# Dissolving the coefficient stage of a graph network kernel into the first softmax

## The chip, the cores and the metric

The kernel runs on one core of one Trainium2 chip. The metric is device time in microseconds of one execution. The kernel before took 5043.83 us, the median of three runs (5041.87 to 5056.84). Engines are named as the profile names them: PE multiplies matrices, DVE is the vector engine, ACT the scalar engine, POOL the GpSimd engine, SP issues DMAs.

## The reference

Four graph layers run over one graph of 50,000 nodes with 128 features and 25,000 edges sorted by destination; each adds its result to its input and normalises it. The first is a three-layer attention network with four heads, then two graph convolutions and a SAGE layer. What the change touches are these lines:

```python
logits = leaky_relu(a_s[src] + a_d[dst] + ew[:, None], 0.2)     # attention; ew: mean of the embedded edge features
                                                                 # self edges take the mean of ew over all edges
deg  = segment_sum(w, col)                                       # convolution 1: weighted degree, self loop of weight 1
dis  = where(deg > 0, rsqrt(deg), 0)
norm = dis[row] * w * dis[col]
deg  = segment_sum(ones, col); norm = rsqrt(deg)[row] * rsqrt(deg)[col]   # convolution 2
m    = segment_sum(h[src], dst) / maximum(deg, 1)                # SAGE
```

## The kernel before, in words

Edges are padded to 25,088 and lie in 196 tiles of 128 slots, 49 batches of four tiles; 98 rows of 256 slots are the second layout of the same edges, in which the softmax scans along the free axis. Nodes are 98 batches of 512.

`program` (line 128) calls one stage after the other: `edge_structure`, `layer_weights`, `node_chain`, `first_slots`, `coefficients`, then `edge_scores(0)`, `softmax(0)`, `attend(0)`, the same three for layers 1 and 2, and five `convolve` stages. Each stage is a block in which every engine has its own instruction list in the order written; lists wait for each other only by semaphores. At a stage's end the semaphores are cleared and all engines meet at a barrier (line 117), so nothing of a stage starts before everything of the stage ahead has ended.

`coefficients` (lines 502 to 555) works alone between two barriers. Its inputs are `ew` (the edges' mean embeddings, [128, 3, 196], for three layers) and `node_map`, which holds for each slot the row number, the weighted degree, the plain degree and a spare column for the edge's source (`src_map`) and for its destination (`dst_map`); one node_map entry is 16 bytes. DVE sums `ew` and adds the bias mean `be1`; PE turns `ew` into the row layout (six transposes) and sums it over partitions with a matrix of ones; DVE rounds the source rows to integers (`src_row`, the gather indices), then makes the masks, one reciprocal, waits for ACT's square root of all degrees, takes their reciprocal, multiplies them into `meta` (coefficients `coef[0..2]` and the self-loop ones), and last writes `ew_mean` and the three `ew_rows` from PSUM.

`edge_scores(0)` gathers source rows with 196 indirect DMAs that POOL issues (line 1434) by `src_row`, paced by PE's progress. `softmax(0)` (line 1756) is a chain on DVE: SP loads the self scores and the edge scores; POOL adds `ew_rows` to the edge scores (line 1834); DVE runs segmented maxima and sums by scans forward (line 274) and backward (line 279), with two short turns through PE (lines 299, 301) in each of three rounds, masks and joins (line 291), and ends with reciprocals and products into `meta` (lines 1899, 1902). `attend(0)` copies `meta` for each batch. The coefficients are first read by the `convolve` stages.

Of the kernel before, what the change touches and what calls it, by code (L numbers as in the profile page):

```python
# [8 lines left out]
F32 = mybir.dt.float32  # L9
I32 = mybir.dt.int32  # L10
ALU = mybir.AluOpType
ACT = mybir.ActivationFunctionType
AX = mybir.AxisListType

P = 128
# [8 lines left out]
ROW = 256  # L24
QUAD = P // GB
STEP = QUAD // HEADS
KEY, COEF, SELF, ALPHA = 2, 3, 6, 8
# [120 lines left out]
def program(nc, io, n_nodes, n_edges):  # L148
    nb, n_slots, n_rows_nodes = sizes(n_nodes, n_edges)
    n_tiles = nb * GB  # L150
    n_rows = n_slots + n_rows_nodes
    rq = n_tiles // 2
    ctx = ExitStack()
    with ctx:
# [16 lines left out]
        ident = sb("ident", [P, P])  # L171
# [3 lines left out]
        src_row = sb("src_row", [P, n_tiles], I32)  # L175
# [3 lines left out]
        meta = sb("meta", [P, n_tiles, 12])  # L179
        w_edge = sb("w_edge", [DE, 3])  # L180
        be1 = sb("be1", [P, 3])
        ones = sb("ones", [P, P])
        ew_rows = sb("ew_rows", [rq, 3, ROW])
# [126 lines left out]
        def edge_structure():  # L310

            with ExitStack() as c, Semaphores(nc) as sem:
# [23 lines left out]
                with nc.Block() as block:  # L336
# [68 lines left out]
                    def _(dve):  # L405
# [92 lines left out]
                        st(nc.vector.tensor_scalar(w_edge[:, :], w_edge[:, :], 1.0 / D, None, ALU.mult))  # L498
                        st(nc.vector.tensor_reduce(be1[:, :], bem[:, :, :], AX.X, ALU.add))
                        st(nc.vector.tensor_scalar(be1[:, :], be1[:, :], 1.0 / D, None, ALU.mult))  # L500

        def coefficients():

            with ExitStack() as c, Semaphores(nc) as sem:
                ew_sum = c.enter_context(nc.sbuf_tensor("ew_sum", [P, 4], F32))
                chain, roots, to_pe, turned = (sem(x) for x in ("chain", "roots", "to_pe", "turned"))
                deg, pos_deg = node_map[:, :, :, 1:3], node_map[:, :, :, 3]
                coef = [meta[:, :, COEF + k] for k in range(3)]
                with nc.Block() as block:
                    @block.scalar  # L510
                    def _(act):
                        act.wait_ge(roots, 1)
                        nc.scalar.sqrt(deg, deg).then_inc(roots, 1)

                    @block.tensor
                    def _(pe):
                        pe.wait_ge(to_pe, 1)
                        nc.tensor.matmul(bank[7][:, 0:3], ones[:, :], ew_sum[:, 0:3], start=True, stop=True)
                        for k in range(3):
                            for j in range(2):  # L520
                                ins = nc.tensor.transpose(bank[k][0:rq, j * P:(j + 1) * P],
                                                          ew[:, k, :].rearrange("p (q j) -> p j q", j=2)[:, j, :], ident[:, :])
                        ins.then_inc(turned, 1)

                    @block.vector
                    def _(dve):
                        st = Chain(dve, chain).step

                        st(nc.vector.tensor_reduce(ew_sum[:, 0:3], ew[:, :, :], AX.X, ALU.add))
                        for k in range(3):  # L530
                            st(nc.vector.tensor_scalar(ew[:, k, :], ew[:, k, :], be1[:, k:k + 1], None, ALU.add))
                        dve.sem_inc(to_pe, 1)
                        st(nc.vector.tensor_copy(src_row[:, :], src_map[:, :, 0]))

                        w_deg = node_map[:, :, :, 1]
                        st(nc.vector.tensor_scalar(pos_deg, w_deg, 0.0, None, ALU.is_gt))
                        st(nc.vector.tensor_tensor(w_deg, w_deg, pos_deg, ALU.mult))
                        st(nc.vector.scalar_tensor_tensor(w_deg, w_deg, 1.0, pos_deg, ALU.add, ALU.subtract))

                        st(nc.vector.tensor_scalar(coef[2], dst_map[:, :, 2], 1.0, 1.0, ALU.subtract, ALU.max))  # L540
                        st(nc.vector.reciprocal(coef[2], coef[2]))
                        dve.sem_inc(roots, 1)
                        dve.wait_ge(roots, 2)
                        st(nc.vector.reciprocal(deg, deg))
                        st(nc.vector.tensor_tensor(w_deg, w_deg, pos_deg, ALU.mult))
                        for k in range(2):
                            st(nc.vector.tensor_tensor(coef[k], src_map[:, :, 1 + k], dst_map[:, :, 1 + k], ALU.mult))
                            st(nc.vector.tensor_tensor(meta[:, :, SELF + k], dst_map[:, :, 1 + k], dst_map[:, :, 1 + k], ALU.mult))
                        st(nc.vector.tensor_tensor(coef[0], coef[0], w_part[:, :], ALU.mult))
                        dve.wait_ge(turned, 1)  # L550
                        st(nc.vector.scalar_tensor_tensor(ew_mean[:, :], bank[7][:, 0:3], 1.0 / n_edges, be1[:, :],
                                                          ALU.mult, ALU.add))
                        for k in range(3):
                            st(nc.vector.tensor_copy(ew_rows[:, k, :], bank[k][0:rq, 0:ROW]))

        def layer_weights(w_first, b_first, beta_col, bias):

# [669 lines left out]
        def edge_scores(l, first, second, t_in, t_mid, t_out, start, end, solo=False):  # L1227
# [3 lines left out]
            with ExitStack() as c, Semaphores(nc) as sem:  # L1231
# [15 lines left out]
                if first:  # L1247
# [13 lines left out]
                sc_stored = [sem(f"sc_stored{r}") for r in range(4)]  # L1261
                x_in, mid_stored, z_stored = ([[sem(f"{n}{h}{r}") for r in range(4)] for h in range(2)] for n in (
                    "x_in", "mid_stored", "z_stored"))
                w_in, tails_out, banks_open, sp_pace, dve_pace = (sem(x) for x in ("w_in", "tails_out", "banks_open", "sp_pace", "dve_pace"))
                n_w = 4 if first else 2
                b_t = bank[0:2]
# [13 lines left out]
                with nc.Block() as block:  # L1280
# [115 lines left out]
                    def _(pool):  # L1396
                        def pace(b, g):
# [20 lines left out]
                            else:  # L1418
                                pool.wait_ge(turned, 2 * b - 1)

                        if patch:
                            for k in range(n_tails):
                                n = min(P, n_tiles - k * P)
                                nc.gpsimd.indirect_dma_start(
                                    out=tails[k][0:n, :], out_offset=None, in_=tables[l].slots,
                                    in_offset=bass.IndirectOffsetOnAxis(ap=tail_index[0:n, k:k + 1], axis=0)).then_inc(tails_in, 16)
                            pool.wait_ge(tails_out, 16 * n_tails)
# [379 lines left out]
        def softmax(layer):  # L1807

            with ExitStack() as c, Semaphores(nc) as sem:  # L1810
# [5 lines left out]
                                     "self_ready", "less_max", "edge_exp", "self_exp"))  # L1816
                summed, edge_turned, sum_turned = (sem(x) for x in ("summed", "edge_turned", "sum_turned"))

                def head_columns(h, j):
                    at = ((h % 2) * 2 + j) * rq  # L1820
                    return slice(at, at + rq)
                with nc.Block() as block:
                    @block.sync
                    def _(sp):
                        for j in range(2):
                            sp.dma_start(sr[:, :, j * P:(j + 1) * P], score_rows(self_score, j)).then_inc(self_in, 16)
                        for j in range(2):
                            sp.dma_start(lr[:, :, j * P:(j + 1) * P], score_rows(edge_score, j)).then_inc(edge_in, 16)

                    @block.gpsimd  # L1830
                    def _(pool):
                        pool.wait_ge(edge_in, 32)
                        for h in range(HEADS):
                            ins = nc.gpsimd.tensor_tensor(lr[:, h, :], lr[:, h, :], ew_rows[:, layer, :], ALU.add)
                        ins.then_inc(edge_ready, 1)

                    @block.scalar
                    def _(act):
                        act.wait_ge(shift_made, 1)
                        act.wait_ge(self_spread, 1)  # L1840
                        for h in range(HEADS):
                            ins = nc.scalar.activation(sr[:, h, :], seg_f[:, h, :], ACT.Identity, bias=shift[0:rq, h:h + 1])
                        ins.then_inc(self_ready, 1)
                        act.wait_ge(less_max, 1)
                        nc.scalar.activation(lr[:, :, :], lr[:, :, :], ACT.Exp).then_inc(edge_exp, 1)
                        act.wait_ge(less_max, 2)
                        nc.scalar.activation(sr[:, :, :], sr[:, :, :], ACT.Exp).then_inc(self_exp, 1)

                    @block.tensor
                    def _(pe):  # L1850
                        for n, what in enumerate(("max", "max", "sum")):
                            run_totals_pe(pe, ends_made, turned, n, what)
                        pe.wait_ge(edge_exp, 1)
# [14 lines left out]
                    def _(dve):  # L1868
                        ch = Chain(dve, chain)
                        st = ch.step  # L1870
                        nc.vector.scalar_tensor_tensor(shift[:, :], att_shift[:, layer, :], -1.0,
                                                       ew_mean[:, layer:layer + 1].to_broadcast([P, HEADS]),
                                                       ALU.mult, ALU.add).then_inc(shift_made, 1)
# [1094 lines left out]
                node_chain(w_first, b_first, beta_col, bias)  # L2968
            first_slots(w_first, b_first, beta_col)
        raw_early.close()  # L2970
        coefficients()
        edge_scores(0, (io["L1_gnn_W1"], io["c_L1_gnn_b1"]), (io["L1_gnn_W2"], io["b_L1_gnn_b2"]), t[3], t[4], t[5], 0, nb)
        softmax(0)
        attend(0)
# [76 lines left out]
```

## Time and profile before

| | |
|---|---|
| median of three runs | 5043.83 us |
| profiled execution, its own time | 5052.05 us |
| its span | 5049.9 us |
| PE busy | 3969.3 us (79%) |
| DVE busy | 3727.1 us (74%) |
| ACT busy | 3450.8 us (68%) |
| POOL busy | 3018.4 us (60%) |
| `coefficients`, from DVE's first instruction to the next stage's first | 1199.76 to 1218.40 us |
| `softmax(0)`, from barrier to barrier | 1606.19 to 1661.94 us |

The share of busy time says little here: the span is a row of stages with barriers between them, and each stage has its own limit. For this change the timeline of two short stretches is what counts. A row of the timeline gives start, duration, engine, line, operation, what is written from what, partitions by elements, how many instructions were merged, and in brackets the engine's idle time before it and what ended that.

### The profile page before, as it was taken

What the parts mean: (1) busy time and instruction counts of PE and PEld (TensorE: products, weight loads), DVE (VectorE), ACT (ScalarE), POOL (GpSimd) and SP (SyncE); (2) the same over time, 40 slices, a digit from 0 to 9 for tenths busy, and PEclk for the clock granted to TensorE, in tenths of its full rate; (3) what the DMA queues carried; (4) which work ended last, traced back from release to release, by engine and by line L of the source; (5) the groups of instructions that cost most, each with busy time, mean ns of one, the idle gap of its engine ahead of it and who ended that gap; (6) DMA issues with size and microseconds to landing.
All of it is one profiled execution on the core that took longest, in us unless ns stands there. A gap on an engine that the chain in (4) does not pass through costs nothing. (4 is left out here: it accounts for less than half of the span.)

```text
span 5049.9 us, 108087 instructions
## 1 busy us (share of the span) xinstructions
PE 3969.3 (79%) x24378; PEld 2916.8 (58%) x24378; DVE 3727.1 (74%) x14651; ACT 3450.8 (68%) x11317; POOL 3018.4 (60%) x2914
## 2 busy tenths in 40 slices
PE   1999999797996898994998974997877666666554
PEld 1667667565774454873555752444766565665554
DVE  4899999545998787897886966997668787544433
ACT  0789999554886676894776863887878787333332
POOL 6888888255452122761224462887757676767777
PEclk9999999798998899997998997998998898997666
DMA  2566666487996576994777984775766565543332
GB/s 90 157 186 200 196 195 197 161 308 258 351 349 220 196 240 203 357 362 146 241 242 243 333 305 141 228 227 169 234 202 208 187 210 187 153 145 115 93 101 70
DMA packets 603571, 1061.32 MB, mean 210 GB/s; under 512 B 109737, under 2 KB 124603, under 8 KB 603373
## 3 DMA queue, kind: packets, MB, share of 16 engines
q1 hardware_dynamic: 521644, 920.61, 53.4%
q0 software_dynamic: 81728, 138.51, 10.6%
q8 instruction: 70, 1.15, 0.1%
q14 instruction: 129, 1.05, 0.1%
HBM read 608.75 MB, written 453.92 MB: 210 GB/s over the span
## 5 line engine op out<-in xcount | busy, mean ns | idle before, releaser
L2540 POOL DMA_INDIRECT got_c<-table,src_row x980 | 931.4, 950 | 387.7 <-issue 311.9
L1434 POOL DMA_INDIRECT src_got_s<-table,src_row x588 | 554.6, 943 | 445.9 <-issue 93.0
L2572 PE MATMUL bank<-pick_c,got_c 128*128 128x128 f32 x1960 | 333.3, 323 | 352.9 <-DMA got_c<-table,src_row 281.5
L2082 PE MATMUL bank<-w_all,dt_m 128*128 128x512 f32 x1176 | 569.2, 601 | 35.2 <-DMA dt_m<-delta_t 34.0
L2572 PEld LDWEIGHTS bank<-pick_c,got_c 128*128 128x128 f32 x1960 | 288.1, 226 | 396.5 <-issue 244.6
L2056 POOL TENSOR_TENSOR part_m<-part_m,half_sum_m 128x512 f32<-128x512 f32 x98 | 158.6, 1619 | 581.8 <-DVE half_sum_m L2289 581.8
L1607 ACT ACTIVATE z_s<-z_s,shift_s,dev_s 128x128 f32<-128x128 f32 x1080 | 444.0, 485 | 2.2 <-DVE shift_s L1745 1.3
L793 PEld LDWEIGHTS bank<-w_mean,ht 128*128 128x128 f32 x2352 | 312.1, 193 | 142.5 <-issue 142.5
L2596 PE MATMUL bank<-w_c,agg_c 128*128 128x128 f32 x1960 | 370.5, 315 | 4.0 <-ACT agg_c L2717 3.8
L2717 ACT COPY agg_c<-bank 128x512 f32<-128x512 f32 x245 | 142.8, 583 | 320.3 <-DVE bank L1920 274.5
L790 PE MATMUL bank<-bias,first_row 128*128 128x512 f32 x588 | 321.3, 628 | 38.0 <-ACT ht L853 13.8
L2082 PEld LDWEIGHTS bank<-w_all,dt_m 128*128 128x128 f32 x1176 | 210.2, 193 | 231.1 <-issue 133.7
L2596 PEld LDWEIGHTS bank<-w_c,agg_c 128*128 128x128 f32 x1960 | 325.1, 230 | 19.8 <-issue 11.5
L843 ACT ACTIVATE bank<-bank 128x128 f32<-128x128 f32 x1176 | 306.8, 261 | 42.0 <-PE bank L793 33.9
L2183 ACT ACTIVATE part_m<-bank,now_m 128x128 f32<-128x128 f32 x588 | 215.0, 366 | 157.7 <-PE bank L2082 141.2
L793 PE MATMUL bank<-w_mean,ht 128*128 128x128 f32 x2352 | 313.2, 277 | 0.0
L2728 ACT ACTIVATE z_c<-z_c,shift_c,dev_c 128x128 f32<-128x128 f32 x588 | 242.2, 482 | 89.0 <-DVE shift_c L2868 89.0
L2832 DVE TENSOR_SCALAR pick_c<-iota,now_c 128x128 f32<-128x128 f32 x980 | 282.3, 365 | 11.8 <-DVE now_c L2828 0.5
L754 POOL TENSOR_TENSOR rows<-rows 128x512 f32<-128x512 f32 x196 | 260.5, 1329 | 42.9 <-DVE rows L925 40.7
L2061 POOL DMA_INDIRECT x_m<-in_x_dram,dst_node x196 | 222.0, 1133 | 98.5 <-issue 52.0
L1913 DVE COPY tails_c<-tails_c 128x1 f32<-128x1 f32 x245 | 37.5, 153 | 328.4 <-PE bank L2572 322.5
L2289 DVE SCALAR_TENSOR_TENSOR part_m<-bank,now_m,part_m 128x128 f32<-128x128 f32 x588 | 203.6, 346 | 69.5 <-ACT half_sum_m L2184 68.2
(352 smaller groups left out, 11912.6 us busy)
## 6 DMA issues: line engine op xcount, KB each, us to landing
table<-rows SPq DMA_DIRECT2D x294, 256.0 KB
x_s<-table SPq DMA_DIRECT2D x270, 256.0 KB
x_c<-table SPq DMA_DIRECT2D x245, 256.0 KB
table<-z_s SPq DMA_DIRECT2D x196, 256.0 KB
table<-z_c SPq DMA_DIRECT2D x196, 256.0 KB
table<-mid_s SPq DMA_DIRECT2D x172, 256.0 KB
own_rows_s<-table SPq DMA_DIRECT2D x147, 256.0 KB
pick_t_s<-picks_t SPq DMA_DIRECT2D x147, 256.0 KB
```

What stands on the lines that cost most here:

```text
L754: nc.gpsimd.tensor_tensor(flat(rows[l + 1][r]), flat(rows[l + 1][r]), flat(rows[l][r]), ALU.add).then_inc(summed[l], 1)
L790: nc.tensor.matmul(b_y[l][:, :], first_row[:, :], bias[:, l, :, :].rearrange("p g d -> p (g d)"), start=True, stop=False, skip_group_check ...
L793: ins = nc.tensor.matmul(b_y[l][:, g * D:(g + 1) * D], ht[l][b.half][:, g, :], w_mean[:, l, :], start=False, stop=True, skip_group_check=True)
L843: ins = nc.scalar.activation(bank[7][:, g * D:(g + 1) * D], b_y[l][:, g * D:(g + 1) * D], ACT.Square, accum_out=square[l][r][:, g:g + 1])
L1434: nc.gpsimd.indirect_dma_start(out=src_got[r][:, g, :], out_offset=None, in_=tables[l].rows, in_offset=bass.IndirectOffsetOnAxis(ap=src_ro ...
L1607: ins = nc.scalar.activation(v[:, g, :], v[:, g, :], ACT.Identity, bias=shift[side(b, h)][:, g:g + 1], scale=dev[side(b, h)][:, g:g + 1])
L2082: nc.tensor.matmul(b_h[k % n_h][:, :], dt[b.slot][:, k, :], w_all[:, l, :, :].rearrange("p h d -> p (h d)"), start=True, stop=True).then_i ...
L2540: nc.gpsimd.indirect_dma_start(out=got[r][:, g, :], out_offset=None, in_=t_in.rows, in_offset=bass.IndirectOffsetOnAxis(ap=src_row[:, t:t ...
L2572: ins = nc.tensor.matmul(b_sum[r][:, k * P:(k + 1) * P], got[b.slot][:, k, :], pick[r][:, k, :], start=k == 0, stop=sage, skip_group_check ...
L2596: ins = nc.tensor.matmul(b_y[r][:, k * D:(k + 1) * D], agg[r][:, k, :], ws[0][:, :], start=False, stop=True, skip_group_check=True)
L2728: ins = nc.scalar.activation(z[b.slot][:, g, :], z[b.slot][:, g, :], ACT.Identity, bias=shift[r][:, g:g + 1], scale=dev[r][:, g:g + 1])
L2832: ins = nc.vector.tensor_scalar(pick[r][:, k, :], iota[:, :], now[r][:, k, KEY:KEY + 1], now[r][:, k, COEF + m:COEF + m + 1], ALU.is_equal ...
```

## The change

`coefficients` is no longer a stage. Its parts go to two later ones:

- In `edge_scores(0)` POOL makes `src_row` itself, waits for it, and then issues the gathers.
- At the head of `softmax(0)` DVE sums `ew` and adds `be1`, PE multiplies and turns into banks 7 and 4 to 6, ACT (instead of DVE) copies the three `ew_rows` out of PSUM, DVE makes `ew_mean`. POOL waits for ACT's copies before its four adds.
- Behind these adds POOL computes all of the degree arithmetic. There is no square root and no reciprocal any more: five tensor_tensor instructions raise to a power, with an exponent of -1 or -0.5 read from a two-column tensor `powers` and broadcast. Each step waits for the one before by a semaphore.

```diff
@@ edge_scores, POOL
+                        if l == 0:
+                            nc.gpsimd.tensor_copy(src_row[:, :], src_map[:, :, 0]).then_inc(rows_known, 1)
+                            pool.wait_ge(rows_known, 1)
@@ softmax, POOL
+                        if layer == 0:
+                            pool.wait_ge(ew_out, 1)
                         pool.wait_ge(edge_in, 32)
                         for h in range(HEADS):
                             ins = nc.gpsimd.tensor_tensor(lr[:, h, :], lr[:, h, :], ew_rows[:, layer, :], ALU.add)
                         ins.then_inc(edge_ready, 1)
+                        if layer == 0:
+                            st = Chain(pool, coef_chain).step
+                            st(nc.gpsimd.memset(powers[:, 0:1], -1.0))
+                            st(nc.gpsimd.memset(powers[:, 1:2], -0.5))
+                            st(nc.gpsimd.tensor_scalar(coef[2], dst_map[:, :, 2], 1.0, 1.0, ALU.subtract, ALU.max))
+                            st(nc.gpsimd.tensor_tensor(coef[2], coef[2], powers[:, 0:1].to_broadcast([P, n_tiles]), ALU.pow))
+                            st(nc.gpsimd.tensor_scalar(pos_deg, w_deg, 0.0, None, ALU.is_gt))
+                            st(nc.gpsimd.tensor_tensor(w_deg, w_deg, pos_deg, ALU.mult))
+                            st(nc.gpsimd.tensor_scalar(w_deg, w_deg, 1.0, None, ALU.add))
+                            st(nc.gpsimd.tensor_tensor(w_deg, w_deg, pos_deg, ALU.subtract))
+                            for part in (src_map, dst_map):
+                                for k in range(2):
+                                    st(nc.gpsimd.tensor_tensor(part[:, :, 1 + k], part[:, :, 1 + k], powers[:, 1:2].to_broadcast([P, n_tiles]), ALU.pow))
+                            st(nc.gpsimd.tensor_tensor(w_deg, w_deg, pos_deg, ALU.mult))
+                            for k in range(2):
+                                st(nc.gpsimd.tensor_tensor(coef[k], src_map[:, :, 1 + k], dst_map[:, :, 1 + k], ALU.mult))
+                                st(nc.gpsimd.tensor_tensor(meta[:, :, SELF + k], dst_map[:, :, 1 + k], dst_map[:, :, 1 + k], ALU.mult))
+                            st(nc.gpsimd.tensor_tensor(coef[0], coef[0], w_part[:, :], ALU.mult))
@@ softmax, ACT
+                        if layer == 0:
+                            act.wait_ge(ew_turned, 1)
+                            for k in range(3):
+                                ins = nc.scalar.copy(ew_rows[:, k, :], bank[4 + k][0:rq, 0:ROW])
+                            ins.then_inc(ew_out, 1)
@@ softmax, PE
+                        if layer == 0:
+                            pe.wait_ge(ew_ready, 2)
+                            nc.tensor.matmul(bank[7][:, 0:3], ones[:, :], ew_sum[:, 0:3], start=True, stop=True)
...
+                            ins.then_inc(ew_turned, 1)
@@ softmax, DVE
+                        if layer == 0:
+                            nc.vector.tensor_reduce(ew_sum[:, 0:3], ew[:, :, :], AX.X, ALU.add).then_inc(ew_ready, 1)
+                            dve.wait_ge(ew_ready, 1)
+                            for k in range(3):
+                                ins = nc.vector.tensor_scalar(ew[:, k, :], ew[:, k, :], be1[:, k:k + 1], None, ALU.add)
+                            ins.then_inc(ew_ready, 1)
+                            dve.wait_ge(ew_turned, 1)
+                            st(nc.vector.scalar_tensor_tensor(ew_mean[:, :], bank[7][:, 0:3], 1.0 / n_edges, be1[:, :],
+                                                              ALU.mult, ALU.add))
@@ program
-        coefficients()
```

POOL in the first softmax, before (L1834 is the add of `ew_rows`, the rows under it end the stage):

```order
L1830 UNCONDITIONAL_BRANCH
L1834 TENSOR_TENSOR edge_r<-edge_r,ew_rows 98x256 x4
L1822 UNCONDITIONAL_BRANCH
L116 ISA
```

```order
L1794 TENSOR_TENSOR edge_r<-edge_r,ew_rows 98x256 x4
L1798 MEMSET powers 128x1
L1799 MEMSET powers 128x1
L1800 ISA
L1800 TENSOR_SCALAR meta<-node_map 128x196
L1801 TENSOR_TENSOR meta<-meta,powers 128x196
L1802 TENSOR_SCALAR node_map<-node_map 128x392
L1803 TENSOR_TENSOR node_map<-node_map 128x392
L1804 TENSOR_SCALAR node_map<-node_map 128x392
L1805 TENSOR_TENSOR node_map<-node_map 128x392
L1808 TENSOR_TENSOR node_map<-node_map,powers 128x196 x4
L1809 TENSOR_TENSOR node_map<-node_map 128x392
```

Sixteen instructions that read the tensors stand behind the adds where there were none; the last five, not shown, are the products L1811 to L1813.

DVE at the head of the first softmax now (before, `self_shift` was its first instruction there, and the three rows ahead of it stood in the coefficient stage):

```order
L1858 UNCONDITIONAL_BRANCH
L1863 TENSOR_REDUCE ew_sum<-ew 128x3
L1866 TENSOR_SCALAR ew<-ew,be 128x196 x3
L1869 SCALAR_TENSOR_TENSOR ew_mean<-bank,be 128x3
L1871 SCALAR_TENSOR_TENSOR self_shift<-att_shift,ew_mean 128x4
L1875 TENSOR_TENSOR self_r<-self_r,tail_bound 98x1024
```

Five DVE instructions come ahead of `self_shift`, the last of them behind a round through PE.

## Rows read from the trace of the kernel before

**Rows 1.** Timeline, the coefficient stage and both barriers around it.
```profile
1196.64 0.50 SPq L1097 DMA_DIRECT2D self_score<-slot_scores  x1
1199.76 0.77 DVE L529 TENSOR_REDUCE ew_sum<-ew 128x3 f32<-128x588 f32 x1 [4.23 <-PEq L117]
1200.56 1.04 DVE L531 TENSOR_SCALAR ew<-ew,be 128x196 f32<-128x196 f32 x3
1201.71 0.50 PEld L518 LDWEIGHTS bank<-ew_sum,ones 128*128 128x128 f32 x2 [6.83 <-DVEq L532]
...
1202.16 1.50 PE L521 MATMUL bank<-ident,ew 128*98 128x128 f32 x6
...
1207.26 5.05 DVE L544 RECIPROCAL node_map<-node_map 128x784 f32<-128x784 f32 x1 [1.01 <-ACT node_map L513]
...
1216.15 1.34 DVE L554 COPY ew_rows<-bank 98x256 f32<-98x256 f32 x3
1218.40 0.20 ACT L1579 ACTIVATE warm<-eps 128x1 f32<-128x1 f32 x1 [11.17 <-SPq L117]
...
1219.04 0.94 POOL L1434 DMA_INDIRECT src_got_s<-table,src_row  x1 [35.79 <-POOLq L117]
```

**Rows 2.** Timeline, first use of a gathered row in edge_scores(0).
```profile
1229.80 1.05 PE L1493 MATMUL bank<-own_rows_s,pick_t_s 128*128 128x128 f32 x8
...
1230.97 0.69 DVE L1712 TENSOR_TENSOR delta_s<-src_got_s,bank 128x512 f32<-128x512 f32 x1 [2.99 <-PE bank L1493]
```

**Rows 3.** Timeline, the head of softmax(0).
```profile
1606.19 1.83 SPq L1826 DMA_DIRECT2D self_r<-self_score  x2
1606.23 0.16 DVE L1871 SCALAR_TENSOR_TENSOR self_shift<-att_shift,ew_mean 128x4 f32<-128x4 f32 x1 [5.44 <-PEq L117]
1608.06 0.94 SPq L1828 DMA_DIRECT2D edge_r<-edge_score  x2
1610.70 1.23 DVE L1875 TENSOR_TENSOR self_r<-self_r,tail_bound 98x1024 f32<-98x1024 f32 x1 [4.31 <-DMA self_r<-self_score]
1611.96 3.88 DVE L274 TENSOR_TENSOR_SCAN seg_f<-pen,self_r 98x256 f32<-98x256 f32 x4
1612.28 4.08 POOL L1834 TENSOR_TENSOR edge_r<-edge_r,ew_rows 98x256 f32<-98x256 f32 x4 [41.08 <-DMA edge_r<-edge_score]
1615.87 2.78 DVE L279 TENSOR_TENSOR_SCAN seg_b<-pen,seg_f 98x256 f32<-98x256 f32 x4
```

**Rows 4.** Windows over edge_scores' and softmax(0)'s stretches: busy time, instructions, granted clock.
```profile
1199.80:1217.50 17.70, 1.94 (x8) 1.48 (x8) 15.90 (x21) 0.89 (x1) 0.00 (x0) 0.50 0.00 0
1217.50:1230.00 12.50, 6.53 (x16) 3.60 (x17) 0.69 (x1) 1.38 (x3) 8.48 (x9) 0.55 0.75 249
1617.00:1661.00 44.00, 4.99 (x22) 3.32 (x22) 39.43 (x68) 5.10 (x7) 0.00 (x0) 0.50 0.00 0
```

**Rows 5.** Lines L274 and L1834: durations in ns, min/median/max.
```profile
L274 DVE TENSOR_TENSOR_SCAN seg_f<-pen,self_r x12: 665/1140/1162, 1612.0 to 3078.6; 98x256 f32<-98x256 f32 x12
L274 DVE TENSOR_TENSOR_SCAN seg_f<-pen,edge_r x12: 666/666/691, 1626.3 to 3092.0; 98x256 f32<-98x256 f32 x12
L1834 POOL TENSOR_TENSOR edge_r<-edge_r,ew_rows x12: 717/1100/1165, 1612.3 to 3079.2; 98x256 f32<-98x256 f32 x12
```

**Rows 6.** Timeline, a DVE instruction beside a POOL add in node_chain.
```profile
186.73 1.70 POOL L754 TENSOR_TENSOR rows<-rows 128x512 f32<-128x512 f32 x1 [0.41 <-DVE rows L925]
...
187.31 1.14 DVE L980 SCALAR_TENSOR_TENSOR shiftn<-statn,devn 128x4 f32<-128x4 f32 x1
```

**Rows 7.** Lines L980, L925 and L754: durations in ns, min/median/max.
```profile
L980 DVE SCALAR_TENSOR_TENSOR shiftn<-statn,devn x98: 123/125/1143, 168.8 to 956.8; 128x4 f32<-128x4 f32 x98
L925 DVE SCALAR_TENSOR_TENSOR rows<-bank,devn,gamma_w x784: 329/336/353, 114.1 to 933.8; 128x128 f32<-128x128 f32 x196
L754 POOL TENSOR_TENSOR rows<-rows x196: 1263/1288/1707, 124.4 to 934.2; 128x512 f32<-128x512 f32 x196
```

**Rows 8.** Timeline, the end of softmax(0) and the start of attend(0).
```profile
1659.63 1.31 DVE L1902 TENSOR_TENSOR meta<-bank,inverse 128x196 f32<-128x196 f32 x2
1661.94 1.28 ACT L2173 ACT_TABLE_LOAD   x1 [20.56 <-PEq L117]
```

More of the change, by code:

```diff
@@ L500, in _ @@
                         st(nc.vector.tensor_scalar(be1[:, :], be1[:, :], 1.0 / D, None, ALU.mult))
[L502 to L554, printed above, removed]
@@ L1263, in edge_scores @@
                     "x_in", "mid_stored", "z_stored"))
+                rows_known = sem("rows_known")
                 w_in, tails_out, banks_open, sp_pace, dve_pace = (sem(x) for x in ("w_in", "tails_out", "banks_open", "sp_pace", "dve_pace"))
@@ L1817, in softmax @@
                 summed, edge_turned, sum_turned = (sem(x) for x in ("summed", "edge_turned", "sum_turned"))
+                if layer == 0:
+                    powers = c.enter_context(nc.sbuf_tensor("powers", [P, 2], F32))
+                    ew_sum = c.enter_context(nc.sbuf_tensor("ew_sum", [P, 4], F32))
+                    ew_ready, ew_turned, ew_out, coef_chain = (sem(x) for x in (
+                        "ew_ready", "ew_turned", "ew_out", "coef_chain"))
+                    deg, pos_deg, w_deg = node_map[:, :, :, 1:3], node_map[:, :, :, 3], node_map[:, :, :, 1]
+                    coef = [meta[:, :, COEF + k] for k in range(3)]
                 def head_columns(h, j):
@@ L1850, in _ @@
                     def _(pe):
+                        if layer == 0:
+                            pe.wait_ge(ew_ready, 2)
+                            nc.tensor.matmul(bank[7][:, 0:3], ones[:, :], ew_sum[:, 0:3], start=True, stop=True)
+                            for k in range(3):
+                                for j in range(2):
+                                    ins = nc.tensor.transpose(bank[4 + k][0:rq, j * P:(j + 1) * P],
+                                                              ew[:, k, :].rearrange("p (q j) -> p j q", j=2)[:, j, :], ident[:, :])
+                            ins.then_inc(ew_turned, 1)
                         for n, what in enumerate(("max", "max", "sum")):
@@ L1870, in _ @@
                         st = ch.step
+                        if layer == 0:
+                            nc.vector.tensor_reduce(ew_sum[:, 0:3], ew[:, :, :], AX.X, ALU.add).then_inc(ew_ready, 1)
+                            dve.wait_ge(ew_ready, 1)
+                            for k in range(3):
+                                ins = nc.vector.tensor_scalar(ew[:, k, :], ew[:, k, :], be1[:, k:k + 1], None, ALU.add)
[3 more added lines that the diff above has]
+                                                              ALU.mult, ALU.add))
                         nc.vector.scalar_tensor_tensor(shift[:, :], att_shift[:, layer, :], -1.0,
```

## The prediction

> **What bounds the kernel now.** The page's chain of waits follows only the last convolution stage and its busy shares are spread over unlike stages, so I read the timeline around the two places that the change touches. There the reader sees a row of stages with barriers. In the coefficient stage DVE works alone: 15.90 us busy of 17.70, PE 1.94, ACT 0.89, POOL and DMA nothing [rows 4]; every microsecond of it is on the path. In softmax(0), behind 1617 us, DVE is busy 39.43 of 44.00 us and POOL not at all [rows 4]: that stage is DVE's chain, and its idle POOL is where the work goes.
>
> **What goes away.** The stage begins for DVE at 1199.76 and the next one for ACT at 1218.40 [rows 1]. All of it goes, one barrier with it: 18.64 us. PE's clock changes nothing: it is granted 0.50 in the coefficient stage and 0.55 just behind [rows 4], so PE starts edge_scores at the lower level (1.2 GHz) in both kernels.
>
> **src_row on POOL.** DVE's cast of 196 elements goes with the stage. POOL's copy has no row; it reads less than the add of 98x256, 0.72 us at its fastest [rows 5], and the wait behind it adds little, so the 196 gathers start about 0.7 us later (0.3 to 1.5). The first gathered row is used at 1230.97, by an instruction that waited for PE [rows 2], while the first gather went out at 1219.04 [rows 1]: the four of batch 0 take about 5 us, landing some us more, and several us of cover remain. Cost 0; without that cover 0.7 us.
>
> **The head of softmax(0).** DVE waited 4.31 us for the self scores, until 1610.70 [rows 3]. New ahead of `self_shift` are the sum and the three adds, which ran from 1199.76 to 1201.60, then PE, whose last transpose ended at 1203.66 [rows 1]: 3.90 us. From the barrier at 1606.23 that is 1610.13; `ew_mean` and `self_shift` at 0.16 us each and their waits end it near 1610.55, 0.1 us before the scores are there. Cost 0, with bounds of 0 and 0.5. ACT's three copies cannot cost DVE's 1.34 us [rows 1] by much more, so `ew_rows` stands by about 1611.6, ahead of POOL's start at 1612.28 [rows 3]. Cost 0, bounds 0 and 0.7.
>
> **POOL's arithmetic.** It runs from 1616.4 (the last add's end) and must be done when DVE is, at 1660.94 [rows 8]. So 44.5 us of time stand open on POOL. The question is what it does to DVE meanwhile.
>
> The trace shows a price [rows 5]. The scans that run beside POOL's adds take 1140 ns in the median, the same scans without them 666; POOL's add goes from 717 to 1100. How it comes about is seen in node_chain [rows 6, 7]: a DVE instruction of 4 elements, 125 ns normally, took 1140 ns and ended at 188.45, when POOL's add, begun at 186.73, had just ended (188.43). It stood still behind a whole POOL instruction. L925, which reads one operand from PSUM, never takes over 353 ns [rows 7]. So a DVE instruction that reads two operands from SBUF waits for a POOL instruction that reads SBUF, to its end. In softmax(0) nearly all of DVE's chain is of this kind (scans, joins, maxima, differences). The Trainium skill states the same as a rule (SBUF — State Buffer, Who interferes with whom): the port pair is an exclusive lock held for the whole instruction, so whoever comes second stands still. It speaks against this change: POOL is idle there, yet its time isn't free.
>
> So each POOL instruction costs DVE about its own streaming time. An add of 256 elements holds about 0.53 us: the difference of the two fastest adds, 1263 and 717 ns for 512 and 256 elements [rows 7, 5], is 2.1 ns an element. Behind the adds stand:
> - two-input plain ones: three of 392 and five of 196 elements, 2,156 x 2.1 ns = 4.5 us;
> - one-input ones: 196 + 2 x 392 = 980 elements at about half, 1.1 us;
> - five powers of 196 elements.
> The plain ones hold 5.6 us. The skill has a rule for these strided operands too (GPSIMD Engine Reference, Performance pitfalls: steps over 8 bytes cost about half more); by it they would be 8.4 us; no row shows it.
>
> No row shows a power on POOL. Lowest: the price of a product, 0.41 us each, 2 us for five. The other end I work out as a program: logarithm, product, exponential are some 30 arithmetic steps; were each as dear as a whole element of an add, 30 x 2.1 = 63 ns an element, 12.3 us an instruction and 62 us for five. An add's element is mostly reading and writing, its arithmetic perhaps a third, which gives 21 ns, 4.1 us each, 20.5 us for five; for comparison, DVE's reciprocal takes 6.4 ns an element [rows 1]. I take 4.1.
>
> DVE's loss is then 5.6 + 20.5 = 26.1 us, less the share that falls on its rounds through PE and its PSUM reads, about 15%: 22.2 us. POOL itself ends near 1616.4 + 5.6 + 20.5 + 16 steps' gaps and waits for DVE (about 10) = 1652.5, before DVE at 1660.9 + 22.2: its own end isn't late. A reload of POOL's library stands ahead of the first tensor_scalar; it falls in POOL's slack. The skill (GPSIMD Engine Reference, Instruction dispatch) puts some 6 us on a freshly loaded kernel's first call; no run here shows it, and by it POOL would still end first.
>
> **Sum.** -18.64 + 0 + 0 + 22.2 = +3.6 us. Against the profiled execution's 5052.05 that is 5055.7. That execution lies 8.2 us over the median of the runs, so I put the difference on the median: 5043.83 + 3.6 = 5047. A measurement of this kernel can hardly tell less than 0.3%, 15.1 us, from no change.
>
> **Rivals.**
> - Slower: the power is dear. Each ns per element of it costs 0.98 us in all, about 0.85 of it on DVE. From 31 ns an element (6 us an instruction) on, the sum passes +15. At the upper end, 63 ns, DVE stands still nearly the whole 62 us: -18.64 + 0.9 x (62 + 5.6) = +42 us, 5086; at twice that, powers taken by code that isn't pipelined, +97, where POOL's end passes DVE's. For it: five times 196 powers in software, and a row that shows whole-instruction blocking. Against it: nothing measured.
> - Faster: POOL's work is hidden after all, because a power computes long and reads little and lets DVE in between, or costs next to nothing, and its plain steps fall on DVE's rounds through PE. The loss must stay under 3.5 us: 5025 to 5029. For it: 44.5 us of open time. Against it: the blocking [rows 5 to 7]; with blocking, even powers at the price of a product leave (5.6 + 2) x 0.8 = 6 us of loss and -12.6 us, 5031, still within 0.3%.
> - The change doesn't do what it says: the head of softmax(0) runs late by the PE round and the ACT copies (1.2 us), or a different wait keeps most of the 18.64 us. 0.5 to 1.2 us only; it moves no case to another.
>
> **How the numbers follow.** The forecast is "within 0.3%" with 5047: powers from 0.4 to 6 us give -12.6 to about +14, its own range 5031 to 5058. Chance 0.47. The slower rival 0.40, the faster one 0.13 (with the third inside these). For 8 in 10 I leave out the lower half of the faster case and the slower case's far tail: 5028 to 5100.
>
> **What the profile after would show.** No DVE row between the last stores of first_slots and the load of edge_scores; ACT's `warm` some 18.6 us earlier. In softmax(0) the tensor_tensor on self_r still at about 4.5 us behind the barrier, its wait ended by the self scores. POOL busy behind its adds with five rows that name `powers`: their duration is the term I know least. Beside them DVE's scans over 666 ns, up to a power's own duration. A scan that keeps 666 ns beside a power refutes the blocking. Softmax(0) longer by about 22 us. The prediction is wrong if softmax(0) grows by less than 3.5 us or more than 34.

## The result and the profile after

The changed kernel takes 5157.07 us (median of four runs, 5148.34 to 5165.25) where the kernel before takes 5046.0 (5041.87 to 5056.84): a ratio of 1.0216, 95% interval 1.0193 to 1.0240. That is 111 us slower; 5047 was forecast, with a range of 5028 to 5100. (The ratios here and below are estimated from all runs of both kernels, and can differ by some 0.1% from the quotient of the two medians.) The kernel is slower beyond doubt; whether by more than 2% the interval leaves open.

The timeline shows the two places where the change acts. First the end of first_slots and the start of edge_scores(0) in the changed kernel (start, duration, engine, line, operation; in brackets the idle time before it), which answers to [rows 1]:

```profile
1180.16 0.50 SPq L1043 DMA_DIRECT2D self_score<-slot_scores  x1
1183.23 0.34 SPq L1230 DMA_DIRECT2D w_s<-in_L_gnn_W_dram  x1
1183.25 0.20 ACT L1529 ACTIVATE warm<-eps 128x1 f32<-128x1 f32 x1 [4.23 <-PEq L117]
1183.27 0.52 POOL L1369 CAST src_row<-node_map 128x196 int32<-128x196 f32 x1 [19.22 <-POOLq L117]
...
1184.06 0.96 POOL L1384 DMA_INDIRECT src_got_s<-table,src_row  x1 [0.27 <-POOL src_row L1369]
```

From the last store's start to ACT's `warm` are 3.09 us; before they were 1218.40 - 1196.64 = 21.76 [rows 1]. So 18.67 us went, as forecast. The gathers start 0.81 us behind `warm` instead of 0.64, and edge_scores(0), from `warm` to the next stage's first load, takes 386.3 us (387.8 before).

Then softmax(0), whose head answers to [rows 3] and whose last row answers to [rows 8]:

```profile
1569.57 0.87 SPq L1784 DMA_DIRECT2D self_r<-self_score  x2
1569.61 0.77 DVE L1863 TENSOR_REDUCE ew_sum<-ew 128x3 f32<-128x588 f32 x1 [5.43 <-PEq L117]
...
1573.23 0.92 ACT L1820 COPY ew_rows<-bank 98x256 f32<-98x256 f32 x3 [7.38 <-PE bank L1839]
...
1573.43 0.16 DVE L1871 SCALAR_TENSOR_TENSOR self_shift<-att_shift,ew_mean 128x4 f32<-128x4 f32 x1
1574.75 1.23 DVE L1875 TENSOR_TENSOR self_r<-self_r,tail_bound 98x1024 f32<-98x1024 f32 x1 [1.16 <-DMA self_r<-self_score]
...
1582.08 32.04 POOL L1801 TENSOR_TENSOR meta<-meta,powers 128x196 f32<-128x196 f32 x1
1582.33 1.01 DVE L279 TENSOR_TENSOR_SCAN seg_b<-pen,seg_f 98x256 f32<-98x256 f32 x1
...
1590.99 2.44 DVE L274 TENSOR_TENSOR_SCAN seg_f<-pen,edge_r 98x256 f32<-98x256 f32 x4
...
1621.06 127.72 POOL L1808 TENSOR_TENSOR node_map<-node_map,powers 128x196 f32<-128x196 f32 x4
...
1624.94 1.32 DVE L1902 TENSOR_TENSOR meta<-bank,inverse 128x196 f32<-128x196 f32 x2
...
1753.05 0.69 POOL L1813 TENSOR_TENSOR meta<-meta,w_part 128x196 f32<-128x196 f32 x1
1754.74 1.28 ACT L2173 ACT_TABLE_LOAD   x1 [148.68 <-PEq L117]
```

A power of 196 elements takes 32 us on POOL. DVE is done at 1626.26, then everyone waits for POOL until 1753.74. From the first load to the next stage's first instruction the stage lasts 185.17 us; before it lasted 55.75 [rows 3, 8]. The balance, +129.4 - 18.7 = +110.7 us, accounts for the 111 between the medians. The two profiled executions themselves are only 96.7 us apart (spans of 5146.6 and 5049.9): the stages ahead, which the change leaves alone, happened to end 16.5 us earlier in the changed kernel's (last store at 1180.16 instead of 1196.64), and what follows softmax(0) took 3.9 us more. So the agreement to 1 us is partly luck; the two lengths above are read inside their stages and don't hang on it.

Two windows, DVE's chain and what is behind it, show who works (the columns are, as in [rows 4]: length, then busy time and instructions of PE, weight loads, DVE, ACT and POOL, the granted clock, the DMA share and GB/s):

```profile
1570.00:1626.30 56.30, 6.93 (x30) 4.80 (x30) 48.42 (x80) 6.02 (x10) 49.37 (x13) 0.50 0.05 15
1626.30:1754.00 127.70, 0.00 (x0) 0.00 (x0) 0.00 (x0) 0.00 (x0) 126.74 (x10) 0.50 0.00 0
```

And DVE isn't slower beside a power: the four scans at 1590.99 take 2.44 us in the middle of one, what the four took before with POOL idle. Only the scan that was issued at the power's start is longer, 1.01 us instead of 0.66 [rows 5]. That refutes the second half of my argument. DVE's chain, from the first load to its last product, takes 56.69 us; before, 54.75. The 1.9 us are 0.7 at the head (the self scores are there 5.2 us behind the load instead of 4.5), 0.6 in the backward scans and 0.6 in the last joins, beside a tensor_scalar of POOL.

### The profile page after: what moved, and what is told of

Read it like the earlier page. It is cut to its first block and busy times, and to the rows that moved or that the text cites. A ratio compares the mean times of both kernels' runs of the same rounds, so it can differ in the third digit from the quotient of the medians.

```text
span 5146.6 us, 108068 instructions
## 1 busy us (share of the span) xinstructions
PE 3930.7 (76%) x24378; PEld 2882.0 (56%) x24378; DVE 3697.7 (72%) x14635; ACT 3449.3 (67%) x11319; POOL 3155.3 (61%) x2933
## 5 line engine op out<-in xcount | busy, mean ns | idle before, releaser
L2596 PE MATMUL bank<-w_c,agg_c 128*128 128x128 f32 x1960 | 353.5, 304 | 5.2 <-ACT agg_c L2717 5.1
L2596 PEld LDWEIGHTS bank<-w_c,agg_c 128*128 128x128 f32 x1960 | 309.7, 220 | 22.1 <-issue 11.5
L2061 POOL DMA_INDIRECT x_m<-in_x_dram,dst_node x196 | 190.2, 970 | 98.4 <-POOLq L117 46.6
```

The costliest lines, as they stand in the source:

```text
L2596: ins = nc.tensor.matmul(b_y[r][:, k * D:(k + 1) * D], agg[r][:, k, :], ws[0][:, :], start=False, stop=True, skip_group_check=True)
```

## The experiments

Theory A, formed from these rows: the loss is the powers' own length, nothing else; beside them DVE runs free. Against it stood B (the new order, the head or the waits cost) and the theory on record, that every POOL instruction which reads SBUF stops DVE for its whole length. The length of softmax(0) below is always from SP's first load to ACT's first row of the next stage. The edits are shown abridged, some lines of them in words.

### Products in place of the powers

```diff
-...to_broadcast([P, n_tiles]), ALU.pow))
+...to_broadcast([P, n_tiles]), ALU.mult))
```

> The changed kernel with each of the five powers turned into a product of the same shape, so the degree powers and coefficients are not computed. Theory A (the powers' own length is the whole loss; beside them DVE runs free): softmax(0) falls from 185.2 us to 57 to 61 us, its end set by DVE again, POOL's sixteen instructions done in about 17 us, and the kernel takes 14 to 17 us less than before (about 5030). Theory B (the loss is the new order: waits, the barrier behind POOL, the head of the stage): softmax(0) stays over 80 us and the kernel is slower than before.

The kernel leaves out the powers, so it doesn't compute the coefficients; it serves for the time alone. 5041.75 us against 5051.87 of before, measured together, ratio 0.9984 (0.9970 to 0.9999): 10 us less by the medians, where 14 to 17 were expected. The rows of its softmax(0):

```profile
1581.64 0.85 SPq L1784 DMA_DIRECT2D self_r<-self_score  x2
...
1601.06 2.87 POOL L1808 TENSOR_TENSOR node_map<-node_map,powers 128x196 f32<-128x196 f32 x4
...
1606.85 4.29 DVE L274 TENSOR_TENSOR_SCAN seg_f<-pen,edge_r 98x256 f32<-98x256 f32 x4
...
1644.66 1.28 ACT L2173 ACT_TABLE_LOAD   x1 [20.58 <-PEq L117]
```

The stage lasts 63.02 us, 122 less than with powers and 7.3 more than before; 57 to 61 was expected, so A's "nothing else" is too strong. B falls as the cause of the loss: the same list in the same order, with products for powers, isn't slower than before. But the plain instructions do cost: the four scans that took 2.44 us now take 4.29. Of the eleven plain instructions the changed kernel ran one ahead of the first power, four beside the last 12 us of DVE's chain, where it mostly waits and reads PSUM, and the six products behind its end; here nearly all run beside scans and joins.

### Powers as logarithm and exponential on ACT

```diff
+ # POOL: masks ahead of its adds, then products once ACT is done
+ # ACT, behind the copies of ew_rows:
+ act.wait_ge(masked, 1)
+ nc.scalar.activation(coef[2], coef[2], ACT.Ln)
+ nc.scalar.activation(deg, deg, ACT.Ln).then_inc(logged, 1)
+ act.wait_ge(logged, 1)
+ nc.scalar.activation(coef[2], coef[2], ACT.Exp, scale=-1.0)
+ nc.scalar.activation(deg, deg, ACT.Exp, scale=-0.5).then_inc(raised, 1)
```

> The changed kernel with the masks on POOL ahead of its adds, and the powers made by ACT as a logarithm and an exponential (784 and 196 elements each), where ACT waits for DVE's first round; only the six products stay on POOL behind the adds. Theory A: ACT needs about 5 us with two table loads (the later table load for the softmax's Exp goes away), all beside DVE; softmax(0) takes 57 to 61 us and the kernel 14 to 17 us less than before. Theory B (any of this work in softmax(0) costs, since POOL's plain instructions stop DVE): softmax(0) over 64 us, gain under 10 us.

5038.28 us, ratio 0.9978 (0.9966 to 0.9989): the first complete version whose whole interval lies below the time before, by 0.1 to 0.3%. ACT's four instructions and both table loads take 6.1 us and end at 1600.52, 11.6 us behind the stage's first load:

```profile
1588.93 0.85 SPq L1783 DMA_DIRECT2D self_r<-self_score  x2
...
1596.96 0.89 ACT L1819 ACTIVATE node_map<-node_map 128x784 f32<-128x784 f32 x1
1597.87 1.28 ACT L1821 ACT_TABLE_LOAD   x1
...
1599.62 0.90 ACT L1822 ACTIVATE node_map<-node_map 128x784 f32<-128x784 f32 x1
1600.20 4.38 DVE L279 TENSOR_TENSOR_SCAN seg_b<-pen,seg_f 98x256 f32<-98x256 f32 x4
...
1648.44 1.28 ACT L2174 ACT_TABLE_LOAD   x1 [20.60 <-PEq L117]
```

The stage lasts 59.51 us, within what A expects. The 3.8 us over before lie beside POOL's plain instructions: 2.3 in the first eight scans, such as the 4.38 us above, which were 2.78 before [rows 3], 0.9 at the head beside the masks, and 0.5 in a copy of four columns.

### Powers and long adds of chosen shapes

```diff
+ # before's kernel, behind the adds; results unused
+ softmax(0): 5 x tensor_tensor(probe, flat_w, flat_w, ALU.add)      # 128x1536
+ softmax(1): tensor_tensor(..., ALU.pow) on 128x384, 128x196, 128x98, 128x49
+ softmax(2): pow on 128x98 (exponent 2), 128x98 (base 1.0), 64x98, 16x98, 8x98, 1x98, 128x196 (exponent 2)
```

> The kernel before with added POOL instructions on scratch tensors behind the adds, results unused: in softmax(0) five adds of 128x1536, in softmax(1) powers of 128 partitions by 384, 196, 98, 49 elements, in softmax(2) powers of 98 elements with exponent 2, of base 1.0, on 64, 16, 8 and 1 partitions, and 128x196 with exponent 2. Theory A (a power is scalar code, one partition's element after the other within a core of 16 partitions): 62.5, 31.9, 16, 8 us; 64 and 16 partitions as dear as 128, 8 partitions half, 1 partition a sixteenth. Theory C (it is vector code over a core's partitions, merely long): every partition count the same. On DVE: if any POOL instruction that reads SBUF stops it for its whole length, each add of 3.2 us costs DVE about 3 us and scans of over 3 us appear in softmax(0), and a power would stop it for 8 to 62 us; if only streaming stops it, the adds stop DVE and the powers cost it under 1 us each, as the one scan of 1.01 us in the changed kernel suggests.

```profile
2322.62 61.63 POOL L1845 TENSOR_TENSOR probe<-gamma_w,expo 128x384 f32<-128x384 f32 x1
2384.33 31.61 POOL L1845 TENSOR_TENSOR probe<-gamma_w,expo 128x196 f32<-128x196 f32 x1
2416.02 15.99 POOL L1845 TENSOR_TENSOR probe<-gamma_w,expo 128x98 f32<-128x98 f32 x1
2432.09 8.15 POOL L1845 TENSOR_TENSOR probe<-gamma_w,expo 128x49 f32<-128x49 f32 x1
...
3159.47 16.11 POOL L1845 TENSOR_TENSOR probe<-gamma_w,expo 128x98 f32<-128x98 f32 x1
3175.65 16.00 POOL L1845 TENSOR_TENSOR probe<-ones,expo 128x98 f32<-128x98 f32 x1
3191.73 16.16 POOL L1845 TENSOR_TENSOR probe<-gamma_w,expo 64x98 f32<-64x98 f32 x1
...
3224.03 15.99 POOL L1845 TENSOR_TENSOR probe<-gamma_w,expo 8x98 f32<-8x98 f32 x1
3240.09 15.99 POOL L1845 TENSOR_TENSOR probe<-gamma_w,expo 1x98 f32<-1x98 f32 x1
```

One run, 5218.29 us. The length is 160 ns an element of the free axis (61.63 - 8.15 us over 335 elements) plus 0.3 us, whatever the partitions and the base; with the exponent it differs by 2% at most (196 elements: 31.6 to 31.9 us with -0.5, 31.6 with 2, 32.0 with -1). One partition costs what 128 cost: C holds, and the scalar-code reading (half for 8 partitions, a sixteenth for one) is wrong. So only the elements along the free axis count, and the changed kernel's tiles already use all 128 partitions.

What the two kinds of instruction do to DVE is seen in single scans, which take about 0.66 us undisturbed. First the five long adds with a scan and a copy beside them, then a scan at the start of the power of 384 elements, and one at the start of the power of 98:

```profile
1611.43 14.89 POOL L1850 TENSOR_TENSOR probe<-w_all 128x1536 f32<-128x1536 f32 x5
1611.63 3.16 DVE L279 TENSOR_TENSOR_SCAN seg_b<-pen,seg_f 98x256 f32<-98x256 f32 x1
...
1621.00 2.53 DVE L281 COPY ends<-seg_b 98x4 f32<-98x4 f32 x1
```
```profile
2322.82 1.24 DVE L279 TENSOR_TENSOR_SCAN seg_b<-pen,seg_f 98x256 f32<-98x256 f32 x1
```
```profile
3159.66 0.77 DVE L279 TENSOR_TENSOR_SCAN seg_b<-pen,seg_f 98x256 f32<-98x256 f32 x1
```

The adds of 3.01 us stop a scan for 2.5 us each, and softmax(0) grew by 11 us (66.78). They stop a copy with one operand too: `ends<-seg_b`, 0.17 us in the kernel before, takes 2.53. A power of 61.63 us stops one scan for 0.58 us, one of 32.04 us (changed kernel, 1.01 us) for 0.35, one of 16.11 us for 0.11 (at the start of the next such power four joins took 0.19 us more), and nothing behind that. From 98 to 384 elements the stop grows by 1.6 ns an element, near an add's price of 2.1, while the length grows by 160. The simplest reading is that a power takes its operands in at its start, then computes with the port free; that inner order is inferred, and three stops are few to give a price by.

### The degree part as a stage again

```diff
+        coefficients()      # src_row, masks, square root, reciprocals, products on DVE and ACT, as before
-        # POOL: src_row in edge_scores(0), the degree arithmetic in softmax(0)
```

> The changed kernel with the degree part undone: a coefficient stage of src_row, masks, square root, reciprocals and products on DVE and ACT as before, while the edge means and rows stay in softmax(0) on DVE, PE and ACT. Theory A: the stage shrinks from 18.9 us by the sum, the three adds, the ew_mean and the three copies (0.77 + 1.04 + 0.16 + 1.34 us and their gaps, 3.5 us) to about 15.4 us; softmax(0) grows by 0 to 1 us, so 2.5 to 3.5 us less than before, within noise. Theory B (the head of softmax(0) is what costs): softmax(0) grows by over 3 us.

5045.21 us, ratio 0.9993 (0.9983 to 1.0003), no change that can be told. Its trace tells more: the stage runs from DVE's first row to ACT's `warm` in 15.02 us, 3.6 less than 18.64, and softmax(0) takes 55.18 us (1596.51 to 1651.69), 0.6 less than before.

```profile
1194.99 0.33 DVE L518 CAST src_row<-node_map 128x196 int32<-128x196 f32 x1 [4.23 <-PEq L117]
...
1210.01 0.20 ACT L1559 ACTIVATE warm<-eps 128x1 f32<-128x1 f32 x1 [9.58 <-PEq L117]
```

The sum and the rows at the head of softmax(0) are free, as predicted.

### Late products, early masks, one power

```diff
+ pool.wait_ge(summed, 1)        # late products: POOL's six products wait for DVE's last two-operand sum
```
```diff
- masks at the head of softmax(0)
+ masks in edge_scores(0), POOL, behind the last gather    # early masks, with late products
```
```diff
- nc.scalar.activation(coef[2], ...Ln), (...Exp, scale=-1.0)
+ nc.gpsimd.tensor_tensor(coef[2], coef[2], powers[:, 0:1]..., ALU.pow)    # one power, with late products
```

> As the kernel with logarithm and exponential on ACT, but POOL's six products wait until DVE has made its last sum from two SBUF operands, so they run beside DVE's reciprocals and products of PSUM data. If only POOL's streaming beside DVE's two-operand instructions costs: softmax(0) falls from 59.5 us to 56.5 to 57.5 us, still ended by DVE; the six products take about 5 us, each at its undisturbed length (0.88, 0.92, 0.54 us). If what costs is the length of POOL's list or a late start, it stays at 59.5 us or grows.

> As the one with late products, and the masks and the clamped degree (five POOL instructions) moved behind the last gather of edge_scores(0), where POOL is idle for some 30 us and DVE reads PSUM in most instructions. edge_scores(0) keeps 386 to 388 us; softmax(0) takes 55.5 to 56.5 us, what it took before; in all 18 us less than before (about 0.36%). If the masks disturb edge_scores(0), that stage grows by 1 us or more.

> As the one with late products, but the one power with exponent -1 is back on POOL behind its adds (32 us), the other four stay on ACT. If a power costs only what it sticks out of the stage: it ends before DVE's last sum, and softmax(0) is as long as in the kernel without it, within 0.6 us. If a power stops DVE or slows it in another way, softmax(0) grows by 3 to 32 us.

All three were measured together, with before at 5056.83 us. Late products: 5041.83, ratio 0.9976 (0.9960 to 0.9992), softmax(0) 57.40 us (59.51 without the delay). Early masks: 5036.73, ratio 0.9969 (0.9957 to 0.9981), softmax(0) 55.71 us, what it took before, with all degree arithmetic beside it or ahead of it:

```profile
1548.24 1.31 POOL L1390 TENSOR_SCALAR meta<-node_map 128x196 f32<-128x196 f32 x1
...
1583.56 1.30 SPq L1791 DMA_DIRECT2D self_r<-self_score  x2
...
1639.27 1.28 ACT L2176 ACT_TABLE_LOAD   x1 [20.61 <-PEq L117]
```

POOL's five masks took 7.5 us from 1548.24 on, and edge_scores(0) wasn't longer than in the changed kernel (386.4 us from `warm` to the next stage's first load, 386.3 there). Early masks is the version I would keep; its interval overlaps the other two, only the stage's rows rank them.

One power, softmax(0)'s start, POOL's power, its first product, and the end:

```profile
1580.17 0.85 SPq L1784 DMA_DIRECT2D self_r<-self_score  x2
...
1592.07 32.15 POOL L1805 TENSOR_TENSOR meta<-meta,powers 128x196 f32<-128x196 f32 x1
...
1628.04 0.92 POOL L1808 TENSOR_TENSOR node_map<-node_map 128x392 f32<-128x392 f32 x1 [3.83 <-DVE seg_f L1898]
...
1637.93 1.28 ACT L2176 ACT_TABLE_LOAD   x1 [20.61 <-PEq L117]
```

The power ends at 1624.22, 3.8 us before it would be missed, and the stage lasts 57.76 us against 57.40 without it: a power of 32 us costs 0.4 us where it fits, of which 0.35 are in the scan at its start. The kernel takes 5037.28 us, ratio 0.9966 (0.9950 to 0.9982). One fits, five don't.

## Why the prediction was wrong

- **The stage that goes**: -18.64 forecast, -18.67 measured. Right.
- **src_row on POOL**: 0 forecast; the gathers start 0.17 us later and edge_scores(0) isn't longer. Right.
- **The head of softmax(0)**: `self_shift` done by 4.0 us behind the barrier, 4.3 forecast; the self scores still end the wait, ACT's copies are 2 us ahead of POOL's adds. The stage with this part alone was not longer, 55.18 us. Right.
- **The size of a power**: this is the step that failed. I took 21 ns an element, 4.1 us an instruction, and wrote that the upper end was 63 ns; it is 160 ns, 32 us. The upper end was built from a guess of 30 arithmetic steps at an add's full price, which no row carried, and no run shows the 30 steps or the third that I took for arithmetic. The trace had no bound above, and a range that ended at 5100 claimed one.
- **The plain instructions**: 5.6 us forecast. Undisturbed they take 11.6, from the rows of the kernel with one power: 6.3 for the two-input ones (4.5 forecast) and 5.3 for the three one-input ones (1.1 forecast). With no power in the list POOL would still have been done in time.
- **What decides from which size on**: for the slower case I let DVE pay 0.9 of the powers' length by blocking and mentioned POOL's end only for twice the upper end. Even that was a wrong sum: by my own terms POOL would end there near 1616 + 130 + 10 = 1756 us and DVE near 1661 + 0.9 x 130 = 1778. As long as DVE pays nine tenths of every power, no total of powers up to some 340 us puts POOL last, so the path that happened was missing from the prediction. With the true size this mechanism would have given -18.64 + 0.9 x (160 + 5.6) = +130 us; 111 was measured, and near as it looks it would be right for a wrong reason. DVE stood still for 0.35 us beside the first power and not at all for the other four, of which one began beside its last PSUM reads and three behind its end. The end is POOL's: it had 44.5 us, needed 160 us for powers alone, and finished 127.5 us behind DVE.
- **The blocking**: right for plain instructions, though one-operand copies are stopped as well, and wrong for a power. With products in the powers' place I forecast 6 us of loss; the stage grew by 7.3 us. The Trainium skill's rule (SBUF — State Buffer, Who interferes with whom: whoever issues first holds the shared port pair for the whole instruction) agrees with the 3.16 us scans beside adds of 3.01 us. It doesn't agree with the powers: 32 us of instruction, 0.35 us of standstill. The measurement decides; how long an instruction reads and writes, as far as that can be inferred from the stops, is what counts here.
- **The rivals**: "slower: the power is dear" is what happened, with the wrong bound and the wrong way of paying. "Faster" named the right fact, that a power computes long and lets DVE in between, and drew the wrong end from it, since it didn't ask how long. The threshold of the slower rival was off too: at 31 ns an element the sum with the 0.85 used there is (30.4 + 5.6) x 0.85 - 18.64 = +12 us, not +15, which is small beside the 160 measured.

## What to carry to other kernels

An operation that no row shows has no upper bound: give it one from a run of its own, or leave the range open. Ask two separate questions of work put on an idle engine: does it fit the time until the barrier, and does it stop a neighbour while it streams; a power on POOL fails the first, plain two-operand instructions the second. Plain POOL work belongs where DVE reads PSUM or waits: here the end of the softmax (2.1 us saved) and the tail of the gathers (1.7 us more). In this kernel the root and the reciprocal were best placed on ACT as logarithm and exponential, since ACT was idle there.

## What was not expected of the hardware

- A power on POOL takes 160 ns an element of the free axis, 76 times an add's 2.1, independent of partitions (1 to 128) and base (1.0 or not), and nearly so of the exponent (-0.5, -1, 2).
- It stops a two-operand DVE instruction only at its start: 0.11 us for 98 elements, 0.35 for 196, 0.58 for 384.
- A plain POOL instruction stops a one-operand DVE copy between SBUF tensors too: 2.53 us instead of 0.17 beside adds of 3.01 us.
- POOL's tensor_scalar of 392 strided elements took 1.93 to 2.17 us, its tensor_tensor of the same tile 0.88 to 0.91 where undisturbed: the one-operand form was the dearer by more than twice. I had priced it at half.
- ACT takes 0.89 and 0.90 us for logarithm and exponential of 784 elements, and 1.28 us for the table load ahead of each, where DVE's reciprocal of the same tile takes 5.05 us [rows 1].
